# Cross-attention and routed experts on one core: attention blocks without engine loops, norms applied by ScalarE, keys and values loaded once a batch, new orders

## The reference, cut to what matters

```python
x = x + attention(_layernorm(x), ctx, ...)      # 16 heads of 32, keys and values from ctx
x = x + ffn(_layernorm(x), ...)
# ffn: of 8 experts, the 2 with the highest router probability; each 512x512,
#      their outputs (x @ W_e.T + b_e) are added up, weighted by the probabilities
```

## Time and profile before

| | us |
|---|---|
| median of 3 runs | 1368.04 (1366.86 to 1373.51) |
| the profiled execution | 1366.51, of it 1364.8 from the first instruction to the last |
| PE busy / PE weight loads | 1227.5 / 743.6 |
| DVE / ACT / POOL busy | 860.4 / 636.1 / 883.1 |
| mean granted TensorE clock | 0.953 of full |

### The profile page before, as it was taken

The page is one execution under the profiler, slowest core; times in us unless marked ns, Lnnn a source line. Parts: engine busy times, 40 slices in busy tenths (PEclk is TensorE's granted clock), DMA queues, the critical chain, the costliest instruction groups (busy, mean ns, idle before and its releaser), DMA issues. The chain is left out here.

```text
span 1364.8 us, 37333 instructions
## 1 busy us (share of the span) xinstructions
PE 1227.5 (90%) x11552; PEld 743.6 (54%) x11553; DVE 860.4 (63%) x1905; ACT 636.1 (47%) x914; POOL 883.1 (65%) x1124
## 2 busy tenths in 40 slices
PE   5696899999998999899999997777899999999997
PEld 3352666665665656666566565443455555555553
DVE  3363687877787678687688676744455555555544
ACT  2204557546655645754754753512333343433333
POOL 5112467878878878878878966966544555454445
PEclk9787899999999989999999998888999999999999
DMA  8814456537647647656654655677999999899786
GB/s 238 224 35 128 116 152 193 188 119 232 200 127 226 179 137 221 173 166 191 193 181 126 209 156 164 243 278 185 245 178 171 173 175 175 167 168 179 143 160 120
DMA packets 136024, 240.07 MB, mean 176 GB/s; under 512 B 18533, under 2 KB 49509, under 8 KB 134757
## 3 DMA queue, kind: packets, MB, share of 16 engines
q1 hardware_dynamic: 102432, 160.67, 40.1%
q0 software_dynamic: 29952, 67.73, 24.4%
q10 hardware_dynamic: 3525, 10.06, 2.0%
HBM read 113.34 MB, written 101.71 MB: 158 GB/s over the span
## 5 line engine op out<-in xcount | busy, mean ns | idle before, releaser
L1778 PE MATMUL S<-we_s,wq_s 128*128 x1632 | 379.5, 383 | 13.9 <-DVE wq_s L1734 5.8
L1711 POOL DMA_INDIRECT out<-xn,to x136 | 210.6, 1549 | 210.1 <-DMA out<-xn,to 80.6
L1111 POOL TENSOR_TENSOR we_s<-P_s,we_s 128x1024 f16<-128x1024 f32 x112 | 239.3, 2155 | 51.2 <-ACT we_s L876 25.5
L1778 PEld LDWEIGHTS S<-we_s,wq_s 128*128 128x128 f16 x1632 | 159.2, 99 | 183.6 <-issue 24.7
L1722 ACT ACTIVATE wq_s<-PVp 128x512 f16<-128x512 f32 x138 | 82.1, 596 | 238.6 <-PE PVp L1768 238.3
L925 DVE TENSOR_REDUCE mx_sb<-S 128x6 f32<-128x924 f32 x160 | 170.9, 1110 | 2.1 <-PE S L684 2.1
L702 PE MATMUL W<-wo_s,aT_hi 128*128 128x512 f16 x512 | 162.7, 384 | 3.6 <-DVE xR_s L935 2.1
L667 PE MATMUL W<-we_s,wq_s 128*128 128x512 f16 x512 | 162.2, 389 | 3.2 <-DVE we_s L913 1.6
L1202 POOL DMA_INDIRECT dispatched<-xn,idx x128 | 126.6, 989 | 47.6 <-issue 46.7
L1756 DVE SCALAR_TENSOR_TENSOR att<-S,be_s 128x512 f32<-128x512 f32 x136 | 94.1, 692 | 97.9 <-PE S L1778 97.0
L768 PE MATMUL PVp<-Vr,we_s 128*128 128x132 f16 x768 | 92.9, 234 | 42.9 <-POOL we_s L1111 42.2
(11 more groups left out here) (190 smaller groups left out, 2038.0 us busy)
## 6 DMA issues: line engine op xcount, KB each, us to landing
P_s<-dispatched SPq DMA_DIRECT2D x140, 260.5 KB, 3.6
we_s<-we_s SPq DMA_DIRECT2D x192, 128.0 KB, 4.0
be_s<-in_x SPq DMA_DIRECT2D x16, 1024.0 KB, 9.7
xR_s<-in_x SPq DMA_DIRECT2D x16, 1024.0 KB, 6.1
out<-xR_s SPq DMA_DIRECT2D x16, 1024.0 KB, 10.4
wst<-in_weT SPq DMA_DIRECT2D x16, 512.0 KB, 7.5
we_scratch<-wsp SPq DMA_DIRECT2D x16, 512.0 KB, 6.9
Kst<-k_scratch SPq DMA_DIRECT2D x16, 480.0 KB, 5.7
```

Source lines behind the costliest of these rows:

```text
L1111: e.tensor_tensor(Pst[1][:, r:r + 2, :], exps(n), Pst[0][:, r:r + 2, :], ALU.subtract).then_inc(pldp, 1)
L1711: e.indirect_dma_start(out, bass.IndirectOffsetOnAxis(ap=to[u][:, :], axis=0), yw[u % YW], None, bounds_check=N - 1, oob_is_err=False, com ...
L1778: m = e.matmul(Yp[:, u % 2, :], gT[u % 2][xp][:, k, :], we_s[:, bass.ds(n * WN + (wp * KC + k) * D, D)], start=(c == 0), stop=(c == 11))
```

## The change

- `slots` writes every slot out; no engine loop is left in the block stage, and nearly all `hold`s of that stage go.
- The norms are applied by ACT (`act_NX`, `act_NY`), one ACTIVATE a tile with scale and bias from `nrm`; `pool_norm_apply` and `pool_NA` go. A ready norm is now counted as four (`nap`).
- `sp_KV` loads only for the first two blocks of a batch.
- LA multiplies the high part with both parts of the weights at once (4 products with 16 columns) and the low part with the high weights (4 with 8): 8 products a row group for 12. `lga` is twice as wide, and `pool_RC` adds its halves where it copied.
- New orders for all five engines and new bank sequences. PE's slot is shifted by one block in number. POOL's BX is split: tile 0 behind PL3, tiles 1 to 3 behind the next block's PL4. SN 1 to 3 and Oe 3 move behind DMX10, ahead of NM 2. ACT applies the norms between PH9 and MTe, with WEh among them. WL, WEh and WEl run one block earlier: in SP's order WL of block 0 and 1 stands ahead of RS of block 0.
- `EARLY = 13`, so the first table has 96 tiles and is worked out one block earlier, and ACT loads it with the first experts.
- SP loads the rows of tiles 0 and 1 ahead of experts 5 to 7. PE has O3..O5, the transposes of tiles 0 and 1, O6..O11, tile 0, LB of block 15, tiles 1 to 6, R of block 15. POOL has SC and SD of block 14 first, then adds with NC, RQ, RP, RW, SC and SD of block 15 between them over 16 tiles.
- The spare rows are stored one a turn in turns 2 to 9.

```diff
-EARLY = 14
+EARLY = 13
...
-    def pool_norm_apply(e, n, b, src, dst):
-
+    def act_apply(e, n, b, j, src, dst):
         e.wait_ge(nco[n], b.at(NCO, NCO))
-        hold(e)
-        for j in range(NJ):
-            i = e.tensor_scalar(dst[:, j, :], src[:, j, :], nrm[n][:, 5, j:j + 1], nrm[n][:, 6, j:j + 1], ALU.mult, ALU.add)
-        i.then_inc(nap[n], 1)
-
+        e.activation(dst[:, j, 0:D], src[:, j, :], ACT.Identity, scale=nrm[n][:, 5, j:j + 1],
+                     bias=nrm[n][:, 6, j:j + 1]).then_inc(nap[n], 1)
+
+    def act_NX(e, b, j):
+        if j == 0 and b.past(1):
+            e.wait_ge(t1p, b.at(4))
+        act_apply(e, 0, b, j, xA[b.par], xn1)
...
         for j in range(NJ):
-            seqs = [t for k in range(KC) for t in split3(k)]
-            for n, (xp, wp, k) in enumerate(seqs):
-                m = e.matmul(W[:, bank, j * NE:(j + 1) * NE], xnT[xp][:, k, j * P:(j + 1) * P], wr_s[:, wp, k, :],
-                             start=(n == 0), stop=(n == 11))
+            o = W[:, bank, j * 2 * NE:(j + 1) * 2 * NE]
+            for k in range(KC):
+                e.matmul(o.rearrange("p (l e) -> p l e", l=2), xnT[0][:, k, j * P:(j + 1) * P], wr_s[:, :, k, :], start=(k == 0), stop=False)
+            for k in range(KC):
+                m = e.matmul(o[:, 0:NE], xnT[1][:, k, j * P:(j + 1) * P], wr_s[:, 0, k, :], start=False, stop=(k == KC - 1))
...
     def sp_KV(e, b):
-        p = b.par
+
+        if b.c % 4 > 1:
+            return
+        p, bt = b.par, b.c // 4
...
-    def slots(e, slot, least, most, per=2):
-
-
-        first, last, lo = -most, NB - 1 - least, 2 - least
-        n = (NB - most - lo) // per
-        for s in range(first, lo):
-            slot(e, Blk(s))
-        with e.Fori(0, n) as it:
-            for k in range(per):
-                slot(e, Blk(lo + k, it, per))
-        for s in range(lo + per * n, last + 1):
+    def slots(e, slot, least, most):
+
+        for s in range(-most, NB - least):
             slot(e, Blk(s))
...
             e.wait_ge(ld_t[0], 16)
-            for u in range(2 * XG):
+            for u in range(2):
                 sp_load(e, 0, u)
+            load_experts(e, 5, NE)
+            for u in range(2, XG):
+                sp_load(e, 0, u)
+            sp_turn(e, 0)
             sp_XS(e, LAST)
...
+            with e.Fori(0, NE) as n:
+                sp_turn(e, n + 2)
+                sp_zero_rows(e, n)
...
+            for i in range(3, 6):
+                pe_O(e, LAST, i, LAST + (-(-2)))
             e.wait_ge(ld_t[0], 16)
+            e.wait_ge(nmd, 4 * NB)
+            pe_turn_rows(e, 0, 0)
+            pe_turn_rows(e, 0, 1)
+            for i in range(6, 12):
+                pe_O(e, LAST, i, LAST + (-(-2)))
             e.wait_ge(ld_ew, 16 * (NE + 1))
...
+            pe_tile(e, 0, 0)
+            pe_LB(e, LAST, LAST + (-(-2)))
+            for u in range(1, TU):
                 pe_tile(e, 0, u)
-                if u == 3:
-                    pe_R(e, LAST, LAST + (-(-2)))
+                if u == 6:
+                    pe_R(e, LAST, LAST + (-(-3)))
```

More of the change, by code:

```diff
@@ new lines, in pe_slot @@
+        if on_b:
+            pe_LA(e, b, s)
+        if on_bm1:
+            pe_ST(e, bm1, 5, s)
+        if on_bm2:
+            pe_AT(e, bm2, 1, s)
+            pe_AT(e, bm2, 2, s)
+        if on_bm1:
+            pe_PV(e, bm1, 0)
+            pe_ST(e, bm1, 6, s)
+        if on_bm2:
+            pe_AT(e, bm2, 3, s)
+        if on_bm1:
+            pe_PV(e, bm1, 1)
+        if on_bp1:
+            pe_XT(e, bp1, 0, s)
+        if on_bm2:
+            pe_O(e, bm2, 0, s)
+            pe_O(e, bm2, 1, s)
+            pe_O(e, bm2, 2, s)
@@ new lines, in pe_slot @@
+        if on_bm1:
+            pe_ST(e, bm1, 7, s)
+            pe_ST(e, bm1, 8, s)
+        if on_bp1:
+            pe_XT(e, bp1, 1, s)
+            pe_XT(e, bp1, 2, s)
+        if on_bm1:
+            pe_PV(e, bm1, 2)
+            pe_PV(e, bm1, 3)
+            pe_ST(e, bm1, 9, s)
+        if on_bm3 and not bm3.last:
+            pe_R(e, bm3, s)
+        if on_bm2 and not bm2.last:
+            pe_O(e, bm2, 3, s)
+        if on_bp1:
+            pe_XT(e, bp1, 3, s)
+        if on_bm2 and not bm2.last:
+            pe_O(e, bm2, 4, s)
+            pe_O(e, bm2, 5, s)
@@ new lines, in pe_slot @@
+        if on_b:
+            pe_MX(e, b, 0, s)
+            pe_MX(e, b, 1, s)
+        if on_bm2 and not bm2.last:
+            pe_O(e, bm2, 6, s)
+        if on_bp1:
+            pe_Q(e, bp1, 0, s)
+        if on_b:
+            pe_MX(e, b, 2, s)
+        if on_bp1:
+            pe_Q(e, bp1, 1, s)
+        if on_b:
+            pe_MX(e, b, 3, s)
+        if on_bm2 and not bm2.last:
+            pe_O(e, bm2, 7, s)
+        if on_b:
+            pe_MX(e, b, 4, s)
+        if on_bm2 and not bm2.last:
+            pe_O(e, bm2, 8, s)
@@ new lines, in pe_slot @@
+        if on_b:
+            pe_MX(e, b, 5, s)
+        if on_bp1:
+            pe_Q(e, bp1, 2, s)
+        if on_b:
+            pe_MX(e, b, 6, s)
+        if on_bm1:
+            pe_PV(e, bm1, 4)
+        if on_b:
+            pe_MX(e, b, 7, s)
+        if on_bp1:
+            pe_Q(e, bp1, 3, s)
+        if on_b:
+            pe_MX(e, b, 8, s)
+        if on_bm2 and not bm2.last:
+            pe_O(e, bm2, 9, s)
+        if on_b:
+            pe_MX(e, b, 9, s)
+        if on_bm2 and not bm2.last:
+            pe_O(e, bm2, 10, s)
@@ L1300, in pe_slot @@
+        if on_b:
+            pe_MX(e, b, 10, s)
+        if on_bm2 and not bm2.last:
+            pe_O(e, bm2, 11, s)
+        if on_bm1:
+            pe_PV(e, bm1, 5)
+        if on_b:
+            pe_MT(e, b, s)
+        if on_bp1:
+            pe_Q(e, bp1, 4, s)
+            pe_Q(e, bp1, 5, s)
+        if on_bm2 and not bm2.last:
+            pe_LB(e, bm2, s)
+        if on_bm1:
+            pe_PV(e, bm1, 6)
+        if on_b:
+            pe_ST(e, b, 0, s)
             pe_ST(e, b, 1, s)
@@ L1473, in act_slot @@
         if on_b:
+            act_EX(e, b, 8)
             act_PH(e, b, 7)
+            act_PH(e, b, 8)
+        if on_bp2:
+            act_XTh(e, bp2, 3)
+        if on_b:
+            act_EX(e, b, 9)
+        if on_bp3 and not bp3.first:
+            act_norm(e, 0, bp3)
+        if on_b:
+            act_PH(e, b, 9)
+        if on_bm2 and not bm2.last:
+            act_NY(e, bm2, 0)
+        if on_bp2:
+            act_WEh(e, bp2)
+        if on_bm2 and not bm2.last:
+            act_NY(e, bm2, 1)
+        if on_bp3:
+            act_NX(e, bp3, 0)
+        if on_bm2 and not bm2.last:
+            act_NY(e, bm2, 2)
+            act_NY(e, bm2, 3)
+        if on_bp3:
+            act_NX(e, bp3, 1)
+        if on_bp2:
+            act_Qh(e, bp2, 0)
+        if on_bp3:
+            act_NX(e, bp3, 2)
+            act_NX(e, bp3, 3)
+        if on_bp1:
+            act_MTe(e, bp1)
+        if on_bm1 and not bm1.last:
+            act_norm(e, 1, bm1)
+        if on_bp2:
+            act_Qh(e, bp2, 1)
+        if on_bp1:
+            act_EX(e, bp1, 0)
     def dve_slot(e, s):
@@ L1532, in dve_slot @@
             dve_SN(e, bm1, 0)
-        if on_bm2 and not bm2.last:
-            dve_RE(e, bm2)
         if on_bp2:
@@ L1537, in dve_slot @@
             dve_XTl(e, bp2, 2)
+        if on_bm2 and not bm2.last:
+            dve_RE(e, bm2)
         if on_b:
             dve_NM(e, b, 1)
+            dve_PL(e, b, 8)
+        if on_bp2:
+            dve_XTl(e, bp2, 3)
+        if on_bm1 and not bm1.last:
+            dve_Oe(e, bm1, 1)
         if on_bm2 and not bm2.last:
             dve_RI(e, bm2)
-        if on_b:
-            dve_PL(e, b, 8)
-        if on_bm1:
-            dve_Oe(e, bm1, 1)
-            dve_SN(e, bm1, 1)
         if on_bp1:
@@ L1877, in _ @@
                 if u == 3:
+                    for j in range(NJ):
+                        act_NY(e, LAST, j)
+                if u == 6:
                     act_RX(e, LAST)
```

437 lines of the change are left out of this document (150 added, 287 removed), and 8 rows, old and new, of the table BANK.

## The result

The changed kernel takes 1381.49 us (median of 20 runs, 1371.02 to 1388.74), the kernel before 1368.92 beside it; the ratio is 1.0085, 95% interval 1.0073 to 1.0097. The forecast was 1313. The profiled execution has a span of 1380.6 us, 15.8 more than before.

The account below looks back on a forecast made before the run. PE was the bound, paced in the blocks by POOL through two short waits a slot. Terms summed to -55.3 on 1366.51, giving 1311.2, so 1313 after the profile's 1.5 offset; own range 1302 to 1325, wider range 1288 to 1346.

Parts of the forecast that it names:

- start: First block: WL and WEh ahead of the first Q eviction delay it 8 us; +7, bounds 0 and 15.
- ten middle slots: Middle block slots: POOL's waits -20.2, clock -8, loop edge -3.4, LA -4; together -35.6, leaving 46.0 us a slot.
- last block to tile 0: From last maxima write to first expert tile: table off DVE, tile transposes between O groups, LB later; -9.
- tiles: Expert tiles: until 1003, R moved to tile 6 and row stores spread, -15.3; later tiles +2.
- My part on the norms: Middle slots: eight applies a slot leave POOL, 6.0 us, twice PE's wait; ACT takes 5.7 us more.
- the part on BX: Middle slots: three BX, 4.5 us of POOL, go behind PL4, out from before the subtractions that PV2 awaits.
- a new wait in the old one's place: Rival: NM 2 to PV6, or ACT's applies to EX0, keeps some 2 us a slot; 1339 us, chance 0.17.
- The rival on the other side: Slower: ACT's applies delay MTe, MR, ST0 and EX0, 5.7 us a slot over 14 slots; 1393 us, chance 0.06.
- POOL's waits: Ten middle slots: of PE's 30.2 us waiting in PV for POOL's subtractions, 20.2 go, 1.0 a slot stays.
- the clock: Ten middle slots: 8 of the 10.2 us lost to PE's lower clock after waits return; bounds 0 and 10.2.
- No loops: Ten middle slots: PE's one sequencer wait at its loop edge goes, -3.4 us once; other engines' edges 0.
- The first table: In the first of two slots to 844.43: 8.9 us of DVE work arrives, slack hides most; costs 3, bounds 0 and 8.9.

Follow-up runs that it names:

- the fixed kernel: Changed kernel plus one wait: POOL makes a block's four indirect stores only after DVE's Q remainder of group 0, four blocks on; 1313.73 us, 0.9586 of the kernel before.
- experiment 5: Kernel before without engine loops: 1368.92 us; the fixed kernel with both norms applied on POOL: 1335.67; the fixed kernel with the old 12-product router product: 1315.53.
- two tiles: Changed kernel, DVE's Q remainder of group 0 reading two SBUF tiles and a written number, without bias column or PSUM sums; 1376.1 us.
- experiment 6: Loop-free kernel before, stores moved to meet DVE's Q remainder of group 0: 1405.18 us; zero for that remainder's bias column: 1402.53; zero in all four remainders: 1402.79.
- experiment 8: The fixed kernel, first block's rows applied on POOL and first table behind the last probability remainder: 1346.47 us, again 1313.76; rows alone 1313.79; table alone 1313.05.
- the combined version: The fixed kernel with both end edits: first block's rows applied on POOL, first table behind the last probability remainder; 1346.47 us, run again unchanged 1313.76.

## Why the prediction was wrong

The sum on the profiled execution, term by term; the fixed kernel shows what each part is worth in an execution without the stalls (the sums are of the unrounded lengths):

| stretch | forecast | changed | fixed |
|---|---|---|---|
| start | +7 | +10.1 | +12.0 |
| to 250.84 | -0.8 | +0.4 | -4.0 |
| ten middle slots | -35.6 | +4.4 | -46.3 |
| to the last write | -3.6 | +2.1 | +0.3 |
| last block to tile 0 | -9 | +0.6 | -3.3 |
| tiles | -13.3 | -1.9 | -9.9 |
| sum | -55.3 | +15.8 | -51.3 |

- **The step that failed** is the middle slots' -35.6, which came out at +4.4. The wait that it counted as gone did go (POOL's 30.2 us became 3.0); a term that it put at nothing took its place. My part on the norms and the part on BX counted what leaves POOL and which wait of PE goes; neither followed `pool_SC`, which the same diff moves behind PL9, to what DVE runs then. The runs showed there: DVE stands 3.6 us beside the four stores, and PE waits 3.3 us once a slot for the maximum behind it (29.5 us in all). Against the fixed kernel that is 32.7 us of PE's idle time and 18.0 of clock in these ten slots. The two spans lie 67.1 apart as a whole, and part of the rest belongs to the kind of execution, not to the wait. Why DVE stands is open: the operands of the remainder fit, but what differs between the two kinds of execution fits as well.
- **The rivals** named the right kind (a new wait in the old one's place) at the wrong spot: NM 2 to PV6 and ACT's applies ahead of MTe and EX0 cost nothing in the changed kernel's waits. The rival on the other side, 0.06, had ACT as its mechanism. Nothing stood for DVE and POOL getting into one another's way, though the Trainium skill's page named above has them contend, and 0.90 for faster left little room for it.
- **POOL's waits**, -20.2, and the clock, -8: PE's idle time fell by 29.9 us in the fixed kernel (33.9 to 4.0), where I had taken 20.2 and the loop edge's 3.4. The norms' place on ACT alone is worth 469.35 - 449.60 = 19.8, idle time and clock together; that it comes near my -20.2, which was for the norms and BX without the clock, is chance. With the old router product and the clock at 1.00 the slots' products take 448.19 us where they took 462.03: the clock's loss was 13.8, not the 10.2 that I had read from one slot. An apply takes 0.80 us on ACT (I took 0.715, bound 0.65 to 0.9).
- **PE's new order**: I took 1.0 us a slot away from the gain; the slots lost 26.6 us in all even with the norms left on POOL (experiment 5), at a clock of 0.99; with the norms on ACT it came back in full, 1.00.
- **No loops**, -3.4: wrong, 0. The wait stood at PE's edge, but without the edge the slots took as long.
- **LA**, -4: the busy time fell by 2.6 us, the slots by 0.3: PE has that much slack there now.
- **The start**, +7: +10 to +12 (bound 15), mostly for another reason. PE stands 10.3 us at its first transposes for ACT's applied rows, and Q's first product starts at 54.58 where it started at 45.76: 8.8 us, a cost that I had not listed. WEh and two applies ahead of the first eviction, for which I had taken the 7, add only some 2 us (it runs at 61.84 instead of 51.14).
- **The first table**, I took 3 us of 8.9: the slot that has it is 8.1 longer than a middle one in the fixed kernel (53.0 against 44.9), and PE waits 9.7 in it; see the last section. No run leaves the table out.
- **Last block to tile 0** and **tiles**: -3.3 and -9.9 in the fixed kernel, of -9 and -13.3. The signs held; the later order hides less.

The forecast of the time was right for the change with one wait more: 1313 against 1313.73. That is partly luck: the middle slots and the two before them gave 13.9 us more than forecast, the start, the table's slot, the last block and the tiles 18.0 less.

## What to carry to other kernels

When a diff moves GpSimd's indirect stores, look at what VectorE and ScalarE have to start during them: here an engine stood still for up to 3.7 us beside them, and a wait that keeps a frequent meeting apart cost nothing (slots of 44.9 us). And when an experiment makes a stall go away, find a place in the program that the experiment does not touch and that had the stall too. If it is gone there as well, the executions differ, and the edit has proved nothing yet: run both kernels again at one time.

## What the runs showed of the hardware

**A stall that outlives the instruction.** The remainder's own row is not longer (0.74 us in both kernels); it is the next instruction that comes 3.6 us late. In the changed kernel DVE resumes 0.84 to 1.03 us behind the last store in eleven of twelve slots and 0.54 us ahead of its end in one; with two tiles it resumes anywhere from 2.4 us ahead of that end to 0.8 behind it. With the first store nothing happened (twelve slots). In experiment 6 an ACT instruction with its operands in PSUM and one column stood too, some 2.3 us a slot. The Trainium skill (SBUF — State Buffer, Who interferes with whom) says that PE and ACT never wait on anyone; ACT did stand here, but no run shows whether it was for SBUF. Which resource it is stays open, and so does why it happens in some executions and not in others.

**Two short locks beside it**, on the timeline of the fixed kernel, DVE's rows and then POOL's:

```profile
781.23 2.10 DVE L1074 TENSOR_TENSOR tb<-reg,tb 128x8 f32<-128x8 f32 x1
783.37 2.05 DVE L1079 TENSOR_SCALAR tb<-tb 128x8 f32<-128x8 f32 x1
785.46 2.04 DVE L1081 TENSOR_SCALAR tb<-tb 128x8 f32<-128x8 f32 x1
787.53 0.17 DVE L1083 TENSOR_TENSOR took<-tb,scan 128x8 f32<-128x8 f32 x1
...
781.19 6.28 POOL L1112 TENSOR_TENSOR we_s<-P_s,we_s 128x1024 f16<-128x1024 f32 x3
```

These rows are from an execution without the stalls above. Three tiny instructions of the table, 0.17 us by themselves, each last as long as one of POOL's three subtractions (6.28 / 3 = 2.09). Behind them PE waits 9.7 us for the remainder of the probabilities. Moved behind that one, the table met three subtractions again (experiment 8). It goes the other way too: POOL's `nrm` step at 441.70 takes 1.20 us instead of 0.20 beside a DVE instruction of 1.21 us that reads two tiles of SBUF (441.64). The second and third of the table's, with one tile and numbers as operands, show that a second input isn't the only way into this lock.

**One program, two times.** The combined version ran at 1346 and, unchanged, at 1314 us, each in all of its runs. A difference of 2.5% between two kernels that were each measured on one occasion is not yet a difference of the kernels. That holds for the changed and the fixed kernel too, beyond the 35 us between 1381 and the 1346 of the combined version with its wait.
